# The first layer norm's root moves from ScalarE to GpSimd, and the statistics of later batches move between the products of the left/right projection

## The reference

```python
# layer 0: pair_repr is (1, 128, 128, 32)
x = _layernorm(pair_repr, ln1_w, ln1_b)           # (x - m) * rsqrt(v + 1e-5) * w + b over 32 features
left = jax.nn.sigmoid(x @ left1) * (x @ left2)
right = jax.nn.sigmoid(x @ right1) * (x @ right2)
p = jnp.einsum('nsre,nkre->nske', left, right)    # per feature a 128 x 128 x 128 product
p = _layernorm(p, ln2_w, ln2_b)
g = jax.nn.sigmoid(jnp.einsum('nsrz,zy->nsry', x, gate))
q = jnp.einsum('nrse,ez->nsrz', p, out_w) * g
x = residual + q
# layer 1: left, gate and sum-of-right projections of x, their product, an output projection, a layer norm
```

## Time and profile before

| | |
|---|---|
| median of 3 runs | 123.48 us (122.88 to 123.65) |
| the profiled execution | 123.37 us |
| its span | 121.6 us |
| mean granted TensorE clock in it | 0.94 |
| busy: TensorE matmul, weight load | 93.8 us, 71.7 us |
| busy: VectorE, ScalarE, GpSimd | 92.1 us, 73.6 us, 68.9 us |
| last product of the projection stage ends | 44.78 us |

### The profile page before, as it was taken

How to read it: one execution, slowest core, us unless ns; L and a number is a source line. 1 busy time by engine, 2 the same in 40 slices (tenths; PEclk the granted TensorE clock), 3 DMA queues, 4 the chain that set the end, 5 groups by cost and what they waited for, 6 DMA issues and landing times.

```text
span 121.6 us, 1791 instructions
## 1 busy us (share of the span) xinstructions
PE 93.8 (77%) x566; PEld 71.7 (59%) x566; DVE 92.1 (76%) x222; ACT 73.6 (61%) x129; POOL 68.9 (57%) x81
## 2 busy tenths in 40 slices
PE   1965795199879969999192999999999999697000
PEld 1954353067647759954141559897798879596000
DVE  1079999499988872999999636477498989799920
ACT  2245472976997628994136983645998698761100
POOL 5047679606299001790470397958754797995700
PEclk9999999968999999999998599999999999999755
DMA  2799990000000000000000000000000005429796
GB/s 52 137 147 153 144 129 3 0 0 0 5 0 0 0 3 5 0 3 0 0 0 0 0 0 5 0 0 3 0 0 5 0 0 86 66 35 145 109 145 104
DMA packets 33484, 4.51 MB, mean 37 GB/s; under 512 B 33348, under 2 KB 33476, under 8 KB 33476
## 3 DMA queue, kind: packets, MB, share of 16 engines
q1 hardware_dynamic: 32160, 4.06, 23.9%
q10 hardware_dynamic: 1316, 0.35, 1.4%
HBM read 2.31 MB, written 2.10 MB: 36 GB/s over the span
## 4 chain that ended last, share of the span: by engine, by line
PE 41%; DVE 35%; issue 7%; ACT 7%; DMA 4%; DVEq 0%; SPq 0%
PE bank L878 7%; PE bank L966 6%; DVE acc_p L713 6%; PE bank L1009 5%; PE bank L1018 4%; DMA x_tok<-in_x 4%; DVE lr L613 4%; PE bank L980 3%; PE bank L983 3%; PE bank L981 3%; DVE sums L584 3%; PE bank L939 3%; DVE lr L797 3%; ACT sig_lr L435 2%; DVE st L592 2%
## 5 line engine op out<-in xcount | busy, mean ns | idle before, releaser
L878 PE MATMUL bank<-lr_blk,xnT 64*128 64x256 f32 x128 | 20.1, 451 | 5.6 <-DVE lr L613 4.0
L878 PEld LDWEIGHTS bank<-lr_blk,xnT 64*128 64x128 f32 x128 | 13.3, 211 | 9.9 <-ACT xnT L425 5.4
L613 DVE TENSOR_TENSOR lr<-bank,sig_lr 128x512 f32<-128x512 f32 x16 | 15.8, 1045 | 2.9 <-ACT sig_lr L435 2.6
L363 POOL TENSOR_TENSOR x_low<-x1T,x_high 128x512 fp32r<-128x512 f32 x8 | 11.0, 1373 | 12.2 <-ACT x_high L496 12.1
L355 POOL TENSOR_TENSOR t_tok<-p_sb,rstd 128x512 f32<-128x512 f32 x7 | 10.4, 1489 | 4.9 <-DVE rstd L754 4.9
L414 ACT ACTIVATE std<-st,eps 128x16 f32<-128x16 f32 (+4 forms) x14 | 4.4, 318 | 13.6 <-DVE st L599 5.3
L279 POOL TENSOR_TENSOR xc<-x_tok,sums 128x512 f32<-128x512 f32 (+2 forms) x7 | 8.0, 1145 | 7.4 <-DVE sums L577 7.4
L435 ACT ACTIVATE sig_lr<-bank 128x512 f32<-128x512 f32 x16 | 9.5, 599 | 3.9 <-PE bank L878 3.8
L379 POOL TENSOR_TENSOR sq<-lr,row_rep 128x512 f32<-128x512 f32 x7 | 9.8, 1400 | 2.0 <-DVE lr L800 2.0
L966 PE MATMUL bank<-tT,out_blk 128*128 128x512 f32 x16 | 9.2, 659 | 2.2 <-DVE x1T L771 2.2
L371 POOL TENSOR_TENSOR oT<-o_a,rsum 128x512 f32<-128x512 f32 x8 | 8.7, 1088 | 2.6 <-issue 1.9
(11 more groups left out here) (120 smaller groups left out, 244.1 us busy)
## 6 DMA issues: line engine op xcount, KB each, us to landing
x_tok<-in_x SPq DMA_DIRECT2D x14, 128.0 KB, 4.3
out<-sq SPq DMA_DIRECT2D x7, 256.0 KB, 3.3
x_tok<-in_x SPq DMA_DIRECT2D x4, 64.0 KB, 4.4
w_rep<-in_weights ACTq DMA_DIRECT2D x1, 180.5 KB
out<-sq ACTq DMA_DIRECT2D x1, 128.0 KB, 4.6
out<-sq SPq DMA_DIRECT2D x1, 128.0 KB, 4.9
row_rep<-in_rows ACTq DMA_DIRECT2D x1, 32.0 KB, 5.0
```

The costliest lines, as they stand in the source:

```text
L363: nc.gpsimd.tensor_tensor(x1_low[:, c % 2], x1T[:, c % 3], x1_high[:, c % 2], ALU.subtract).then_inc(x1_low_ready, 1)
L613: nc.vector.tensor_tensor(lr[:, :, s].rearrange("p f s -> p s f"), src[:, :, 2 * CH:4 * CH], sig_lr[:, j % 3].rearrange("p (s f) -> p s f" ...
L878: last = nc.tensor.matmul(dst, xnT[half, c, k * P:(k + 1) * P], lr_blk[half].rearrange("p g m c -> p g (m c)"), start=True, stop=True, ski ...
```

## The change

The root and the reciprocal of the first layer norm become one power, (v + eps) to the -0.5, on GpSimd, over `SUMS1`, which now has seven batches: 8, 8, 16, 16, 16, 32 and 32 rows. `ROOTS1` and ScalarE's `root1_of` are gone. ScalarE's very first function is Sigmoid instead of Sqrt. VectorE now makes v itself, with a scalar_tensor_tensor for the difference (times 1/32) and a clip that also adds eps. It no longer interleaves batches: `statistics1(b)` is one batch from end to end. Batches 0 to 3 (48 rows) stand ahead of the first product, batches 4, 5 and 6 behind the first product of chunks 0, 1 and 2. GpSimd's power of a batch stands between its centring and its normalisation; that of batch 0 stands ahead of the wait for the weights. TensorE's transposes 1 and 2 stand between the first two projections; before, transpose 2 stood within the second. The second DMA of batch 0 is issued on ScalarE's queue, ahead of the weights.

```diff
-SUMS1 = [(0, 8), (8, 16), (16, 32), (32, 48), (48, 64), (64, 96), (96, 112), (112, 128)]
-ROOTS1 = [(0, 8), (8, 16), (16, 32), (32, 48), (48, 64), (64, 96), (96, 128)]
+SUMS1 = [(0, 8), (8, 16), (16, 32), (32, 48), (48, 64), (64, 96), (96, 128)]
...
@@ sync
-                    for n in range(2):
+                    for n in range(2 if b else 1):
...
@@ gpsimd
+            nc.gpsimd.memset(minus_half[:], -0.5).then_inc(minus_half_set, 1)
...
+            def root1(b):
+                lo, hi = SUMS1[b]
+                pool.wait_ge(var1, b + 1)
+                v = stat(st[:, 0], lo, hi)
+                half = minus_half[:].rearrange("p (m q) -> p m q", m=1).to_broadcast([P, v.shape[1], v.shape[2]])
+                nc.gpsimd.tensor_tensor(stat(rstd[:, 0], lo, hi), v, half, ALU.pow).then_inc(rstd1, 1)
...
             pool.wait_ge(consts, 1 + 2 * GRP)
+            pool.wait_ge(minus_half_set, 1)
+            root1(0)
             pool.wait_ge(w_in, 16)
...
-            centre(1)
-            for b in range(2, 6):
+            for b in range(1, len(SUMS1)):
                 centre(b)
-                normalise1(b - 1)
-            normalise1(5)
-            normalise1(6)
-            for b in (6, 7):
-                centre(b)
-            for n in (7, 8):
-                normalise1(n)
+                root1(b)
+                for n in [n for n, (lo, hi) in enumerate(TURNS) if holding(SUMS1, lo) == b]:
+                    normalise1(n)
...
@@ scalar
+            lo, hi = SUMS1[0]
+            act.dma_start(place(x_tok[:], lo, hi)[:, 1], x_tok_dram[:, lo + 1:hi:2, :]).then_inc(x_in[0], 16)
             act.dma_start(w_rep[:], weights.rearrange("(a p) n -> a p n", a=1).to_broadcast([GRP, CH, n_w])
...
-            nc.scalar.activation(std[:, 0, 0:1], eps[:], ACT.Sqrt).then_inc(warm, 1)
+            nc.scalar.activation(std[:, 0, 0:1], eps[:], ACT.Sigmoid).then_inc(warm, 1)
             act.wait_ge(warm, 1)
             square1(0)
             square1(1)
-            root1_of(0)
             square1(2)
             act.wait_ge(w_in, 16)
             affine1(0)
-            root1_of(1)
             square1(3)
-            root1_of(2)
+            affine1(1)
+            sigmoid_lr(0, 0)
+            affine1(2)
             square1(4)
-            affine1(1)
-            root1_of(3)
+            sigmoid_lr(0, 1)
+            affine1(3)
             square1(5)
-            affine1(2)
-            root1_of(4)
-            square1(6)
-            root1_of(5)
-            for c in range(CHUNKS):
+            for c in range(1, CHUNKS):
...
                 sigmoid_lr(c, 1)
-                if c == 0:
-                    square1(7)
-                if c == 2:
-                    root1_of(6)
+                if c == 1:
+                    square1(6)
...
@@ vector
+            def variance1(b):
+                lo, hi = SUMS1[b]
+                dve.wait_ge(minus1, b + 1)
+                dve.wait_ge(sumsq1, b + 1)
+                nc.vector.scalar_tensor_tensor(out=stat(st[:, 0], lo, hi), in0=stat(sums1[:, 3], lo, hi),
+                                               scalar=1.0 / CH, in1=stat(sums1[:, 2], lo, hi),
+                                               op0=ALU.mult, op1=ALU.add).then_inc(diff1, 1)
+                dve.wait_ge(diff1, b + 1)
+                nc.vector.tensor_scalar(stat(st[:, 0], lo, hi), stat(st[:, 0], lo, hi), 0.0, EPS,
+                                        ALU.max, ALU.add).then_inc(var1, 1)
+
+            def statistics1(b):
+                add_x(b)
+                mean(b)
+                add_squares(b)
+                variance1(b)
...
+            statistics1(0)
             lo, hi = SUMS1[0]
             dve.wait_ge(mean1, 1)
             nc.vector.tensor_tensor(place(xc[:], lo, hi), place(x_tok[:], lo, hi),
                                     each_feature(sums1[:, 0], lo, hi), ALU.subtract).then_inc(centre0, 1)
+            statistics1(1)
...
                                     each_feature(rstd[:, 0], lo, hi), ALU.mult).then_inc(xn_ready, 1)
+            statistics1(2)
...
             nc.vector.tensor_copy(q_bias[:], bank[:, 7, CH:CH + 1]).then_inc(out0_ready, 1)
+            statistics1(3)
             for c in range(CHUNKS):
                 multiply_lr(c, 0)
+                if c + 4 < len(SUMS1):
+                    statistics1(c + 4)
                 multiply_lr(c, 1)
...
@@ tensor
-                    if j == 1 and n == 1:
-                        transpose_xn(2)
...
+            project_lr(0, 0)
+            transpose_xn(1)
+            transpose_xn(2)
+            project_lr(0, 1)
+            transpose_xn(3)
+            pe.wait_ge(out0_ready, 2)
+            for c in range(1, CHUNKS):
                 project_lr(c, 0)
-                if c == 0:
-                    transpose_xn(1)
-                elif c < CHUNKS - 2:
+                if c < CHUNKS - 2:
                     transpose_xn(c + 3)
                 project_lr(c, 1)
```

More of the change, by code:

```diff
@@ L154, in pair_layers @@
         eps = sb("eps", [P, 1])
+        minus_half = sb("minus_half", [P, 1])
         scratch = sb("scratch", [P, 1])
@@ L187, in pair_layers @@
         mean1, centred1_pool, squared1 = sem("mean1"), sem("centred1_pool"), sem("squared1")
-        var1, root1, rstd1 = sem("var1"), sem("root1"), sem("rstd1")
+        var1, rstd1 = sem("var1"), sem("rstd1")
         xn_ready, xn_pool = sem("xn_ready"), sem("xn_pool")
@@ L191, in pair_layers @@
         step, eps_set, warm = sem("step"), sem("eps_set"), sem("warm")
+        minus_half_set = sem("minus_half_set")
         proj_split, x1_high_ready, x1_low_ready = sem("proj_split"), sem("x1_high_ready"), sem("x1_low_ready")
@@ L281, in centre @@
                                         ALU.subtract).then_inc(centred1_pool, 1)
+            def root1(b):
[4 more added lines that the diff above has]
+                nc.gpsimd.tensor_tensor(stat(rstd[:, 0], lo, hi), v, half, ALU.pow).then_inc(rstd1, 1)
             def normalise1(n):
                 lo, hi = TURNS[n]
-                pool.wait_ge(rstd1, holding(ROOTS1, lo) + 1)
+                pool.wait_ge(rstd1, holding(SUMS1, lo) + 1)
                 pool.wait_ge(centred1_pool, holding(SUMS1, lo) + 1 - OWN_CENTRE)
@@ L410, in root @@
             def root(layer, lo, hi, done):
[L411 to L419, removed]
+                nc.scalar.activation(std[:, layer, lo:hi], st[:, layer, lo:hi], ACT.Sqrt, scale=1.0 / CH,
+                                     bias=eps[:]).then_inc(done, 1)
             def affine1(n):
@@ L577, in mean @@
                 nc.vector.tensor_scalar(stat(sums1[:, 0], lo, hi), sums, 1.0 / CH, None, ALU.mult).then_inc(mean1, 1)
-                nc.vector.scalar_tensor_tensor(out=stat(sums1[:, 2], lo, hi), in0=sums, scalar=-1.0 / CH, in1=sums,
+                nc.vector.scalar_tensor_tensor(out=stat(sums1[:, 2], lo, hi), in0=sums, scalar=-1.0 / CH ** 2, in1=sums,
                                                op0=ALU.mult, op1=ALU.mult).then_inc(minus1, 1)
@@ L630, in _ @@
                                     each_feature(sums1[:, 0], lo, hi), ALU.subtract).then_inc(centre0, 1)
-            add_x(1)
-            inverse1(0)
-            mean(1)
+            statistics1(1)
             dve.wait_ge(centre0, 1)
@@ L649, in _ @@
                                     mask[:], ALU.mult).then_inc(out0_ready, 1)
-            variance1(2, 2)
             nc.vector.tensor_copy(q_bias[:], bank[:, 7, CH:CH + 1]).then_inc(out0_ready, 1)
[L652 to L670, removed]
+            statistics1(3)
             for c in range(CHUNKS):
                 multiply_lr(c, 0)
[L673 to L677, removed]
-                multiply_lr(c, 1)
[L679 to L683, removed]
+                if c + 4 < len(SUMS1):
+                    statistics1(c + 4)
+                multiply_lr(c, 1)
                 if c == 2:
-                    inverse1(6)
                     dve.wait_ge(w_in, 16)
@@ L894, in _ @@
             pe.wait_ge(lr_blk_ready, 1)
-            for c in range(CHUNKS):
-                if c == 1:
-                    pe.wait_ge(out0_ready, 2)
+            project_lr(0, 0)
[5 more added lines that the diff above has]
+            for c in range(1, CHUNKS):
                 project_lr(c, 0)
-                if c == 0:
-                    transpose_xn(1)
-                elif c < CHUNKS - 2:
+                if c < CHUNKS - 2:
                     transpose_xn(c + 3)
                 project_lr(c, 1)
-                if c == 0:
-                    transpose_xn(3)
             pe.wait_ge(blocks, 6)
```

1 line of the change is left out of this document (removed).

## The result

The changed kernel takes 134.97 us in the median of four runs, against 123.19 for the kernel before beside it: 1.091 of its time, 95% interval 1.086 to 1.097. The forecast was 123.2, no change, with a range up to 126.0. The profiled execution has a span of 132.1 us (121.6 before). A kernel here has a faster and a slower state, and all ratios, and all medians from here on, go by the runs in the faster one: that leaves out 136.52 here (134.77 without it), 181.63 in e1, 129.10 and 129.28 in e5 and 130.74 in e6.

What follows compares the result with a forecast made beforehand. Bound: VectorE's statistics up to the first product, then a ring of projection, sigmoid and product. Seventh product 0.5 us earlier, kept to the last, plus 0.3 for TensorE's clock: 123.37 - 0.2 = 123.2 us; range 121.2 to 126.0.

Steps and rivals of the forecast that it cites:

- Added: Seven powers on GpSimd, taken as 0.3, 0.4 and 0.6 us for 8, 16 and 32 columns; ends 0.19 and 1.05.
- the walk: Operation-by-operation estimate of the new order: first half-chunk product at 16.0 us, seventh at 33.5, the sixteenth and last ending at 44.2.
- rival C: GpSimd's power is the new bound, in batches 1 to 3 and before normalisations 7 and 8: 125.2, up to 126.3; 26%.
- the loop of batches 1 to 3: VectorE and GpSimd wait for each other through centring, variance, power, normalisation and mean: 3.05 us per 16 rows.
- rival B: Powers at 0.2 us and VectorE's small operations slipping in between two of GpSimd's: 121.4 us; 28%.
- The ring after M6: Projection, sigmoid, product, projection, from the seventh half-chunk product to the sixteenth and last: 10.7 us, as in the kernel before.
- the prediction's own sign: The forecast fails altogether if the stage after the seventh product doesn't take 10.7 us, for then the ring isn't the limit.
- TensorE's clock: Lower clock level after a 3.5 us gap before the sixth transpose makes later projections late: 0.3 us taken, ends 0 and 0.9.
- Holding: VectorE's short tensor_scalar or tensor_tensor operations end 0.03 us after the GpSimd operation they meet; L689 and L690 both held.
- A reading of before: Table loads at 21.42 and 32.12 are behind the largest of VectorE's gaps before products, 2.6 us of waits for sigmoids.
- The first load: Second half of batch 0 issued on ScalarE's queue: 0.4 us off, batch 0 starting at 6.15; ends 0 and 0.42 off.
- Rival D: The first power on GpSimd stalls and moves its whole queue: some 128 us, or 129 by the skill's 6 us; 4%.

Runs made afterwards that it cites:

- e1: The changed kernel with GpSimd's power replaced by a multiplication over the same elements: 121.43 us, 0.985 of the kernel before.
- e5: The changed kernel with real powers for batches 0 to 4 and multiplications for batches 5 and 6: 127.2 us, 1.028 of the kernel before.
- e6: The changed kernel with multiplications for batches 0 to 3 and real powers for 4, 5 and 6: 128.69 us, 1.046 of the kernel before.
- e2: The kernel before with only the first load changed (second half of batch 0 on ScalarE's queue): 122.98 us against 123.18, ratio 1.001.
- e3: The changed kernel with the first load as in the kernel before: 137.02 us, 1.116 of the kernel before.
- e9: The changed kernel with an exponent of 1 instead of -0.5, one execution: 134.84 us.
- e10: The changed kernel with the exponent in a full tile of 128 columns instead of one column broadcast, one execution: 134.91 us.

## Why the prediction was wrong

- **The step that failed** is "Added": "I take 0.3, 0.4 and 0.6 for 8, 16 and 32 columns". Measured: 1.66, 2.9, 5.42, 22.9 us in all where the walk had 3.0. The upper end, "a full 128x512 pass, 1.05", was no upper end: it was taken from an operation of another kind. Its "16 to 32 times the elements" (64 times for 8 columns) was to leave room for a power's work, but from 16 to 32 columns each column costs 0.157 us, 77 times the 0.002 of a column of that pass. The lower end, 0.19, is what a multiplication of that size takes (0.22 in e1), so the bound was one for the instruction and left the power's own work out. Up to five times the price of the top end made rival C the case, far beyond its 126.3.
- **The mechanism of rival C** was right in kind: GpSimd's powers hold the transposes. It named the loop of batches 1 to 3 and the release of T7 and T8 by batch 6. The first place is shown (e5), but the loop was not the one between two engines that the walk had: centring, power and normalisation, 5.0 us per 16 rows, are GpSimd's list alone, and VectorE isn't in it. The dearest place it did not name is T5, behind the powers of batches 4 and 5: in e6 5.3 of 7.2 us are lost by M5. In the changed kernel T5 waits 4.95 us for its normalisation (3.82 in e1), and T7, behind batch 6's power, 2.11 (not at all in e1). Its 1.05 per power was short by a factor of 1.6 to 5.2.
- **The walk for the order**, with cheap powers, stands up fairly well in e1: M0 at 14.8 (forecast 16.0), M6 at 31.3 (33.5), M15 at 43.0 (44.2). Its time of 121.4 is also that of rival B, whose cheap powers e1 has. But errors cancel in the walk. The 1.2 at M0 are mostly the first load: centring 2 starts at 10.57 instead of 11.8, with only two of the cheap operations ahead of it, 0.5 together where the walk had 0.6. From M0 to M6 it took 16.5, not 17.5, because the two short operations of the output weight were not held as forecast (0.15 and 0.24, not 1.75 together). The ring after M6 took 11.7, not 10.7: sigmoids no longer stood ready, and each transpose in the ring opened a gap of 0.5 to 0.7 in front of a product. In the changed kernel it took 13.8, with the wait for T7 in it. By the prediction's own sign the forecast then fails altogether; the ring was indeed not all that limits this stage.
- **TensorE's clock**: the place was right, as TensorE's timeline in e1 shows. T5 comes behind a gap of 3.82, and four transposes and the sixteen matmuls of P5 and P6 take 1.12 and 3.78, where the earlier trace rows had 1.04 and 3.26. The granted clock is 0.51 in 24 to 27 and 0.50 in 27 to 30, the lower level. M5 at 29.63 doesn't wait for P5, since VectorE has batch 6's statistics until 29.64; M6 waits 0.18 for its sigmoid and M7 0.71. What the clock cost in all was not measured by itself.

```profile
25.83 1.12 PE L813 MATMUL bank<-ident,xc 128*128 128x128 f32 x4 [3.82 <-POOL xc L298]
26.88 3.78 PE L828 MATMUL bank<-lr_blk,xnT 64*128 64x256 f32 x16
```

- **Holding**: normalisation and centring held VectorE's short operations as forecast, the new scalar_tensor_tensor too (L587 at 28.76 took 0.70, until the centring of 27.51 ended). The power did not, though no row of before could say so. The first two of these rows of VectorE's timeline in the changed kernel lie within the power of 13.13 to 16.03 at their usual length:

```profile
14.08 0.17 DVE L587 SCALAR_TENSOR_TENSOR st<-sums 128x16 f32<-128x16 f32 x1
14.28 0.17 DVE L591 TENSOR_SCALAR st<-st 128x16 f32<-128x16 f32 x1
...
28.76 0.70 DVE L587 SCALAR_TENSOR_TENSOR st<-sums 128x32 f32<-128x32 f32 x1
```

  The walk also let GpSimd hold L689, an operation on a single column. In the kernel before that one took 0.15 beside the normalisation of 32.73. It didn't slip in between two of GpSimd's, as rival B had it. In e1 the same operation lies in the middle of a normalisation of 1.05 from 30.04 on and isn't held:

```profile
30.73 0.15 DVE L641 TENSOR_SCALAR wout_mean<-wout_mean 128x1 f32<-128x1 f32 x1
```

- **A reading of before** was off. The table load of 32.12 is not behind one of the largest gaps in front of products: M6 waits 0.23 for its sigmoid, and the second largest gap, 0.60 at 39.87, has no load near it.

- **The first load** was under-sized: batch 0 was there at 3.5 and not at 6.15. In the old order that is worth nothing (e2). In the changed kernel it is worth 2 us (e3), since the first power starts by as much earlier.
- **Rival D**, a stall ahead of the first power, did not occur. The wait of 2.74 before it ends 0.19 after VectorE's variance, as it does before e1's multiplication (5.87), and the first power takes 1.66, no longer than the second. The Trainium skill's GPSIMD Engine Reference, section Instruction dispatch, gives the first call of a freshly loaded kernel about 6 us; the estimate of 129 that went with it has no row here that bears it out.

## What to carry to other kernels

A function that the trace of before doesn't show has no upper bound from rows of other functions. Forecast it with a range of several times the dearest neighbour, and measure it by itself before an order is built around it; the test is cheap: put an operation of the same form in its place and see what the order is worth. Here everything but the power was worth 1.5% and the power cost 11%. And a step that moves to another engine is priced by that engine's list: 21.3 us more on GpSimd (22.9 against e1's 1.6) became 13.3 of the time, because GpSimd's normalisations feed the transposes in order.

## What the runs showed of the hardware

- GpSimd's power costs by the column: 1.66, 2.90 and 5.42 us for 8, 16 and 32 columns of 128 partitions. The differences, 1.24 and 2.52, give 0.155 to 0.158 us per column, and by this 0.4 is left for the instruction. A multiplication of the same form takes 0.22 to 0.24 at 16 and 32 columns (e1). Neither an exponent of 1 (e9) nor the form of the operand (e10) changes it.
- While a power runs, VectorE's short tensor_scalar, tensor_tensor and scalar_tensor_tensor operations pass (0.17 us at 14.08 and 14.28 of the changed kernel). Those of 8 to 32 columns that start while a centring or normalisation runs end with it (0.70 instead of 0.17 to 0.19 at 28.76). A scalar_tensor_tensor with two operands in SBUF is held like a tensor_tensor. An operation on one column was not held (0.15 at 30.73 of e1).
- With the second half of batch 0 issued on ScalarE's queue ahead of the weights, batch 0 is there at 3.5 us (e2), where it took until 6.56 in the kernel before and 6.63 in e3 with both halves on SP's queue beside the weights' transfer. The weights are there 0.9 us later for it (7.40 in e2, 6.52 before). Whether the other queue or the place ahead of the weights does it was not tried.
